# Four graph layers on one core: the edge matrix loaded by GpSimd's converting DMA, small vector steps taken apart, and new orders on every engine

## The reference, cut to what matters

```python
h = jnp.maximum(_layernorm(x), 0.0); x = x + _L0_gnn_ref(h, adj, W, a)        # one-head masked attention
h = jnp.maximum(_layernorm(x), 0.0); x = x + _L1_gnn_ref(h, adj, W, b, a)     # four-head masked attention
h = jnp.maximum(_layernorm(x), 0.0); x = x + _L2_gnn_ref(h, adj, a0..a3, bias)  # sigmoid of h*a0 @ h.T where adj == 1
h = jnp.maximum(_layernorm(x), 0.0); x = x + _L3_gnn_ref(h, adj, weight, ...)   # three rounds of: aggr, then a GRU cell
# L0, L1: e = leaky_relu(s1[:, None] + s2[None, :]); softmax over the neighbours; att @ (h @ W.T)
# L3:     A = (adj != 0).astype(f32); for i in range(3): aggr = A.T @ (h @ weight[i]); h = gru(aggr, h)
```

## Time and profile before

| | |
|---|---|
| Median of 3 runs | 1108.17 us (1105.32 to 1108.45) |
| Profiled execution: time, and span of the core | 1104.81 us, 1103.0 us |
| Busy PE / DVE / ACT / POOL | 959.7 / 944.8 / 885.0 / 96.1 us |
| Steady stretch, busy per 63.0 us | PE 57.6, DVE 58.4, ACT 54.6 us |

### The profile page before, as it was taken

How to read it: one execution, slowest core, us unless ns; L and a number is a source line. 1 busy time by engine, 2 the same in 40 slices (tenths; PEclk the granted TensorE clock), 3 DMA queues, 4 the chain that set the end, 5 groups by cost and what they waited for, 6 DMA issues and landing times.

```text
span 1103.0 us, 16049 instructions
## 1 busy us (share of the span) xinstructions
PE 959.7 (87%) x5024; PEld 613.6 (56%) x5024; DVE 944.8 (86%) x2710; ACT 885.0 (80%) x1876; POOL 96.1 (9%) x138
## 2 busy tenths in 40 slices
PE   4677898989989898998989898998989799898875
PEld 3453655656565565656566565656556465655443
DVE  5396989899898989999898989989898998988543
ACT  3477897979889797979889797988979798887643
POOL 0101010010001010100101011010101100000000
PEclk8678999999999999999999999999999999999989
DMA  2101111020111102011111102011110201101000
GB/s 89 50 37 48 39 48 48 11 86 11 39 49 48 49 11 87 10 41 47 48 49 48 50 10 79 18 40 49 48 49 10 87 1 40 48 1 48 1 10 10
DMA packets 34028, 43.92 MB, mean 40 GB/s; under 512 B 1040, under 2 KB 17424, under 8 KB 33936
## 3 DMA queue, kind: packets, MB, share of 16 engines
q1 hardware_dynamic: 25488, 38.61, 11.1%
q10 hardware_dynamic: 8448, 4.20, 1.3%
HBM read 38.61 MB, written 4.19 MB: 39 GB/s over the span
## 4 chain that ended last, share of the span: by engine, by line
PE 47%; DVE 36%; ACT 7%; issue 6%; POOL 3%; DMA 0%; DVEq 0%; ACTq 0%; SPq 0%; POOLq 0%
DVE probs L611 9%; PE l_bank L879 6%; DVE probs L625 6%; PE x_bank L968 5%; PE a_bank L911 4%; DVE sess L781 3%; PE r_bank L1029 3%; DVE sess L774 3%; PE n_bank L1029 2%; PE n_bank L1044 2%; ACT hn L367 2%; PE n_bank L1047 2%; PE l_bank L934 2%; PE r_bank L1032 2%; PE h_bank L1032 2%
## 5 line engine op out<-in xcount | busy, mean ns | idle before, releaser
L625 DVE SCALAR_TENSOR_TENSOR probs<-spread,s_lift,probs 128x512 f32<-128x512 f32 x320 | 232.9, 746 | 1.8
L611 DVE CUSTOM_DVE_ANT_0 probs<-spread,mask 128x512 f32<-128x512 f32 x320 | 211.9, 684 | 3.4 <-ACT spread L427 3.1
L443 ACT ACTIVATE pT<-l_bank 128x512 f32<-128x512 f32 x256 | 153.7, 600 | 40.9 <-PE l_bank L879 40.9
L435 ACT ACTIVATE probs<-probs,shift_p 128x512 f32<-128x512 f32 x256 | 185.0, 723 | 1.0 <-DVE probs L625 1.0
L879 PEld LDWEIGHTS l_bank<-ident,probs 128*128 128x128 f32 x1024 | 123.8, 144 | 78.8 <-issue 40.5
L879 PE MATMUL l_bank<-ident,probs 128*128 128x128 f32 x1024 | 155.0, 277 | 10.0 <-ACT probs L435 9.1
L349 POOL TENSOR_TENSOR rstd<-var_eps,power 128x4 f32<-128x4 f32 x64 | 72.8, 1137 | 961.0 <-DVE var_eps L605 636.3
L367 ACT ACTIVATE hn<-x,shift,rstd 128x128 f32<-128x128 f32 x192 | 79.4, 498 | 34.6 <-POOL shift L351 34.6
L934 PE MATMUL l_bank<-hT,dst_rep 128*128 128x512 f32 x128 | 72.1, 646 | 12.9 <-ACT pT L443 11.0
L427 ACT ACTIVATE spread<-l_bank 128x512 f32<-128x512 f32 x64 | 38.4, 600 | 42.2 <-PE l_bank L934 42.2
L1015 PE MATMUL y_bank<-hn,sess 128*128 128x128 f32 x512 | 64.3, 279 | 8.3 <-DVE sess L781 8.3
(11 more groups left out here) (174 smaller groups left out, 2010.0 us busy)
## 6 DMA issues: line engine op xcount, KB each, us to landing
adj_i<-in_adj SPq DMA_DIRECT2D x16, 1024.0 KB, 5.1
adjt_i<-in_adj_t SPq DMA_DIRECT2D x16, 1024.0 KB, 5.5
xin<-in_x SPq DMA_DIRECT2D x16, 256.0 KB, 2.9
out<-out_sb ACTq DMA_DIRECT2D x16, 256.0 KB, 4.8
weights_sb<-in_weights SPq DMA_DIRECT2D x1, 840.0 KB, 4.6
```

The source lines that it names most:

```text
L435: s.activation(row, row, ACT.Exp, bias=shift_p[:, head, c:c + 1], accum_out=den[:, head, c:c + 1]).then_inc(probs_ready, 1)
L443: s.activation(pT[:, head - 1, :, c * P:(c + 1) * P], l_banks[unit % 2][:, :].rearrange("p (j i) -> p j i", j=C), ACT.Copy).then_inc(pT_co ...
L611: chain.link(v.tensor_tensor_reduce(out=row, in0=spread_row, in1=mask, scale=1.0 / LIFT, scalar=-3e38, op0=ALU.subtract, op1=ALU.max, accu ...
L625: v.scalar_tensor_tensor(row, spread_row, source, row, ALU.min, ALU.subtract, reverse1=True).then_inc(ready, 1)
```

## The change

Five things:

1. The edges step leaves ACT. POOL issues a DMA per graph that reads adj again from HBM and converts int32 to fp32r on its way into the edges buffer. It waits for the last agg of two graphs before. `load_adj` no longer waits for edges.
2. minus_mean and var_eps move from DVE to POOL, ahead of its pow. DVE's sums step is split in two, stats and aggr, between which other DVE work may stand.
3. max is split into top (above and empty), below and max. top now stands behind the head's first u or v, and the rest behind further ones. The wait for shift_p moves from DVE's first logits to ACT's first exponential of the head.
4. The reciprocals (den0, rden0, den1), the scaling (scaled) and the state (state) become steps of their own, without own waits. norm, sum and sum0 become four steps each.
5. All tables are written anew, for 175 steps in place of 136.

```diff
+L_STEPS = ([... for step in [f"below{n // 4 + 1}"] * (n % 4 == 1) + [f"v{n}"] + [f"top{n // 4 + 1}"] * (n % 4 == 0)
+              + [f"max{n // 4 + 1}"] * (n % 4 == 1) + [f"q{n - 1}"] * (n > 0) + ...
...
-                    sp.wait_ge(edges_ready, p.before().count(1, 1))
...
+                g.tensor_scalar(minus_mean[n][:, :], moments[n][:, :, 0], -1.0, None, op0=ALU.mult)
+                if n < NORMS - 1:
+                    last = g.tensor_scalar(var_eps[n][:, :], moments[n][:, :, 1], EPS, None, op0=ALU.add)
...
+                last.then_inc(pool_step[n], 1)
+                pool.wait_ge(pool_step[n], p.count(2, 1))
                 g.tensor_tensor(rstd[n][:], var_eps[n][:], power[:], op=ALU.pow).then_inc(pool_step[n], 1)
...
+                if step == "edges":
+                    if p.before(2).exists():
+                        pool.wait_ge(agg_ready, p.before(2).count(LAYERS, LAYERS))
+                    g.dma_start(edges[:, p.graph % 2, :, :], rows(adj, p.graph)).then_inc(edges_loaded[p.graph % 2], 16)
...
-                    s.activation(edges[:, p.graph % 2, :, :], adj_i[:, :, :], ACT.Sign).then_inc(edges_ready, 1)
...
+                    if c == 0:
+                        act.wait_ge(shift_ready, p.count(H1, head))
                     act.wait_ge(logits_ready, p.count(UNITS, unit + 1))
...
-                chain.own(last)
+                chain.link(last)
+
+            def moments_of(n, chain):
+                chain.wait()
                 for c in range(C):
                     last = v.bn_aggr(moments[n][:, c, :], stats[n][:, c, :])
-                chain.own(last)
-                v.tensor_scalar(minus_mean[n][:, :], moments[n][:, :, 0], -1.0, None, ALU.mult)
...
+                if part == "top":
+                    dve.wait_ge(max_ready[k], p.count(heads, nth))
+                    v.scalar_tensor_tensor(above[k][:, :], rmax[:, head, :], -1.0, s1_lift[:, head, :], ALU.mult, ALU.add)
+                    v.tensor_scalar(empty[k][:, :], rmax[:, head, :], -2.0, -MASK, ALU.mult,
+                                    ALU.add).then_inc(shift_step[k], 1)
+                elif part == "below":
+                    dve.wait_ge(shift_step[k], p.count(2 * heads, 2 * nth - 1))
...
```

More of the change, by code:

```diff
@@ L20 @@
 PLAIN = 1024.0
-A_STEPS = (["stats0", "norm0", "rows0", "mask0", "dst0", "src0", "values0"] + [f"m{c}" for c in range(4)] + ["max0"]
-           + ["u0", "u1", "t0", "u2", "t1", "u3", "t2", "t3", "sum0", "x1"])
-L_STEPS = (["stats1", "norm1", "count", "rows1", "mask1", "dst1", "edges", "values1"]
-           + [f"n{c}" for c in range(4)] + ["max1", "dst2"]
+A_STEPS = (["stats0", "aggr0"] + [f"norm0_{c}" for c in range(4)] + ["rows0", "mask0", "dst0", "src0", "values0"] + [f"m{c}" for c in range(4)]
+           + ["u0", "top0", "u1", "t0", "below0", "u2", "t1", "max0", "u3", "t2", "t3", "den0", "rden0"] + [f"sum0_{c}" for c in range(4)] + ["x1"])
@@ L27 @@
+L_STEPS = (["stats1", "aggr1"] + [f"norm1_{c}" for c in range(4)] + ["count", "rows1", "mask1", "dst1", "edges", "values1"]
+           + [f"n{c}" for c in range(4)] + ["dst2"]
            + [step for n in range(16)
-              for step in [f"v{n}"] + [f"q{n - 1}"] * (n > 0) + [f"dst{n // 4 + 3}"] * (n in (2, 6))
-              + [f"n{n + 4}"] * (n < 12) + [f"max{n // 4 + 2}"] * (n in (3, 7, 11))] + ["q15"])
-B_STEPS = (["sum", "x2", "stats2", "norm2", "rows2"] + [f"z{n}" for n in range(4)] + ["kinds"]
-           + [f"s{n}" for n in range(4)] + [f"w{n}" for n in range(4)] + ["x3", "stats3", "norm3", "rows3"])
@@ L32 @@
-GATES = (("split", "agg", "hidden_r", "hidden_n", "joint_r", "joint_n", "hidden_z", "joint_z", "mix", "turn"),
-         ("hidden_r", "agg", "hidden_n", "joint_r", "joint_n", "hidden_z", "joint_z", "mix", "turn"))
+              for step in [f"below{n // 4 + 1}"] * (n % 4 == 1) + [f"v{n}"] + [f"top{n // 4 + 1}"] * (n % 4 == 0)
+              + [f"max{n // 4 + 1}"] * (n % 4 == 1) + [f"q{n - 1}"] * (n > 0) + [f"dst{n // 4 + 3}"] * (n in (2, 6))
+              + [f"n{n + 4}"] * (n < 12)] + ["q15"])
@@ new lines @@
+B_STEPS = ([f"sum1_{j}" for j in range(4)] + ["den1", "scaled", "x2", "stats2", "aggr2"]
+           + [f"norm2_{c}" for c in range(4)] + ["rows2"] + [f"z{n}" for n in range(4)] + ["kinds"]
+           + [f"s{n}" for n in range(4)] + [f"w{n}" for n in range(4)] + ["x3", "stats3", "aggr3"]
+           + [f"norm3_{c}" for c in range(4)] + ["rows3"])
+GATES = (("split", "agg", "hidden_r", "hidden_n", "joint_r", "joint_n", "hidden_z", "joint_z", "mix", "state", "turn"),
+         ("hidden_r", "agg", "hidden_n", "joint_r", "joint_n", "hidden_z", "joint_z", "mix", "state", "turn"))
@@ L814, in step_c @@
                     dve.wait_ge(n_ready, p.count(LAYERS, n))
-                    cc.own(v.scalar_tensor_tensor(n_t[:, :], z_t[:, :], -1.0, n_t[:, :], ALU.add, ALU.mult))
+                    cc.link(v.scalar_tensor_tensor(n_t[:, :], z_t[:, :], -1.0, n_t[:, :], ALU.add, ALU.mult))
+                elif step == "state":
+                    cc.wait()
                     v.scalar_tensor_tensor(state[:, layer % 2, :], keep[:, :], 0.5, n_t[:, :], ALU.mult,
```

233 lines of the change are left out of this document (128 added, 105 removed), and 113 rows, old and new, of the table WHEN.

## The result

The changed kernel takes 1129.2 us (median of 4 runs, 1124.4 to 1133.2). The kernel before took 1108.3 us beside it (4 runs, 1105.3 to 1111.0), so the ratio is 1.0188, 95% interval 1.0133 to 1.0242. It is **slower by 1.9%**, where 2.9% less was forecast. The profiled execution took 1126.3 us, with a span of 1124.5.

A forecast was written before the change was run, and what follows sets the result against it. It took a loop through DVE's and PE's queues as the bound: 42.2 + 18.1 + 0.35 + 0.15 = 60.8 us per period, 2.2 less than 63.0; fourteen periods give 31 us off, so 1076 us, range 1050 to 1112.

The forecast's parts named there:

- The loop as counted: Steady loop through DVE and PE: period 60.0 to 61.6 us, time 1062 to 1086 us, chance 0.48.
- the first rival: The outcome with the summed loop holding: period 60.0 to 61.6 us, 1062 to 1086 us, chance 0.48.
- the two stretches: Chain of waits per period: one stretch on DVE, 42.2 us after the change, and one on PE, 18.1 us.
- max taken apart: DVE's four max instructions without stalls: 0.35 us gained per head, 1.4 us per period in the chain's DVE stretch.
- edges off ACT: Frees 1.9 us per period on ACT, counted as nothing in the steady part; -1.5 us once in the fill.
- minus_mean and var_eps on POOL: Norms 0.15 to 0.3 us longer up to shift, up to 1.4 beside DVE; nothing per period, fill and drain +1 us.
- the reserve of norm1: norm1 must be there when PE is done with the sum; counted as having 1.5 us to spare.
- I go by the row: POOL and DVE excluding each other could hold DVE up to 26 us; not counted, as a DVE row took its usual 0.69.
- The slower rival: ACT held at each head's first exponential by shift_p: period 64.6 us, time 1127 us, chance 0.13.
- what would show the forecast wrong: Signs: ACT idle at first exponentials, DVE rows lengthened under POOL, agg waiting for the edges DMA, a chain through the norm.
- The case of 1.4 us per period at a norm: norm1 losing its reserve to the longer way over POOL: 1096 us, within the give-back rival of chance 0.18.

The follow-up runs named there:

- a_norm_dve: The changed kernel with the norm's two small instructions, minus_mean and var_eps, back on DVE, all else kept: 1083.4 us, ratio 0.9731.
- d_pool_norm01: The changed kernel with minus_mean and var_eps on POOL for norm0 and norm1 only, on DVE for norm2 and norm3: 1084.1 us, ratio 0.9737.

## Why the prediction was wrong, step by step

- **The loop as counted.** Without the POOL edit the period is 61.56 us and the time 1083.4, against 60.8 and 1076, just inside the first rival's 60.0 to 61.6 and 1062 to 1086. The sum over the other parts was good to 1%. It had taken all fourteen periods of before for 63.0 us; from 180.35 to 1004.92 they are 63.4 on average, three of them with a lowered stretch. The chain isn't the two stretches that I expected, though: in a_norm_dve it goes over ACT too, between exponentials and tanh.
- **max taken apart**, 1.4 us of the loop per period: measured 1.0 (13.9 us over 14 periods). Mechanism right, size two fifths too large.
- **edges off ACT: nothing.** Right in the old orders where the DMA's wait blocks no norm (0.4% gained at most); 4.0% are lost where it does. The look at POOL's queue in the prediction was needed. The transfer lands after 5.7 us (POOL's issue takes 0.85), where the estimate from the Trainium skill's page "DMA: Bandwidth & Descriptors" (section on the anatomy of a DMA on the GpSimd path) was 4.4; the measurement decides. In no trace does an engine wait for it. That the new orders can't do without it (50 us) I hadn't seen, since load_adj's wait for edges was not in my sum.
- **minus_mean and var_eps on POOL: "I take nothing per period".** This is the step that failed. I had the price, "0.15 to 0.3 us longer up to shift", "up to 1.4" if DVE is in the way. On POOL it measured 2.4 us more at norm2 (4.2 in place of 1.8) and 1.2 at norm3. Counted as I had counted, from the end of bn_aggr to shift, norm2 took 4.3 us in place of 2.15 and norm3 3.15 in place of 2.2, so 2.1 and 0.95 us longer. And I asked for the reserve of norm1 alone, which is the norm with one: d_pool_norm01 shows no cost at norm0 and norm1. norm2 and norm3 have none in the new orders, where their ways make 1.5 us per period at full clock. In the old ones PE already waited 1.2 to 1.4 us for norm3's rows in every steady period. The four norms should have been gone through one by one: what waits behind shift, and when was it last idle.
- **"I go by the row"** for the exclusion of POOL and DVE. The row was right for DVE, which is not held. For POOL the one pow of 2.41 us in the earlier trace rows was not followed further. In the changed kernel the pow of norm2 takes 2.24 or 2.25 us in 11 of the 14 graphs from 169.98 us on, and 1.34 to 1.63 in the others.
- **The clock was not in the sum at all.** The window of the earlier trace rows shows 1.00, and I took it for given, though three of thirteen periods of that same trace are at 0.97. Longer waits of PE took it away more often, for about 1.5 us per period.
- **The slower rival** named ACT at the first exponentials, 0.13. It is refuted: 8.2 us of such waits in the whole run. Its period of 64.6 us is nearly the measured 64.50, by luck (its sum gives 1076 + 14 x 3.8 = 1129 us, not 1127). The right one, a chain that goes through the norm, stood only in the list of what would show the forecast wrong.
- **Range.** 1129 lies above 1112. The case of 1.4 us per period at a norm was priced (1096), but with one norm, not two, and without the clock.

## What to carry to other kernels

A small instruction moved to an idle engine was paid for here in length, not in busy time. Go through every place where the step occurs, and ask at each what waits behind it and which instructions of the other engine run beside it. Where the lengthened way ends in a wait of TensorE, look at the granted clock behind that wait in the trace of before. Undo a part of a compound change by itself before giving up the whole: here the change without one edit is 2.7% faster than the kernel before.
